# A Perceiver layer's scan: a sixth state pair summed on GpSimd, the gated sum behind the third keys, the first pair's products a step later

## The reference, cut to what matters

```
x = x + xattn(layernorm(x), ctx)            # softmax attention, 257 context tokens
h = layernorm(x)
gate = sigmoid(h @ W_gate.T + b_gate)
x_p, delta = split(h @ W_in.T + b_in);  delta = relu(delta)
s[t] = s[t-1] * exp(A * delta[t]) + x_p[t] * delta[t] * B     # 16 states, 512 channels
y[t] = s[t] @ C[0] + x_p[t] * D
x = x + (gate * y) @ W_out.T + b_out
```

## Time and profile before

| | us |
|---|---|
| median of 3 runs | 2247.94 (2247.15 to 2249.84) |
| the profiled execution | 2246.96 |
| its span in the trace | 2245.1 |
| granted PE clock, mean | 0.917 |

### The profile page before, as it was taken

The page is one execution under the profiler, slowest core; times in us unless marked ns, Lnnn a source line. Parts: engine busy times, 40 slices in busy tenths (PEclk is TensorE's granted clock), DMA queues, the critical chain, the costliest instruction groups (busy, mean ns, idle before and its releaser), DMA issues. The chain is left out here.

```text
span 2245.1 us, 41621 instructions
## 1 busy us (share of the span) xinstructions
PE 1864.1 (83%) x14355; PEld 1256.0 (56%) x14355; DVE 1592.2 (71%) x2945; ACT 1475.6 (66%) x3431; POOL 1207.8 (54%) x1300
## 2 busy tenths in 40 slices
PE   4898988988988898899899774378989898888964
PEld 2655555555555555555555432356666666676743
DVE  3348777767867867867858787457788878878763
ACT  2558877777868868867868776124666666656654
POOL 1435555545546545545545633156777767767751
PEclk8999999999999999999999997678889999989876
DMA  7321112112211211111111110100000000000000
GB/s 187 111 90 60 62 55 67 60 54 67 66 56 59 78 59 62 60 61 60 59 52 60 38 47 5 54 7 9 13 12 12 12 12 12 12 12 12 10 8 10
DMA packets 48370, 103.20 MB, mean 46 GB/s; under 512 B 6384, under 2 KB 25072, under 8 KB 43376
## 3 DMA queue, kind: packets, MB, share of 16 engines
q1 hardware_dynamic: 48240, 101.57, 14.4%
HBM read 93.03 MB, written 8.52 MB: 45 GB/s over the span
## 5 line engine op out<-in xcount | busy, mean ns | idle before, releaser
L861 POOL TENSOR_TENSOR kcube<-kcube,ksq 128x512 f32<-128x512 f32 x128 | 178.0, 1391 | 487.2 <-ACT ksq L718 487.2
L696 ACT ACTIVATE abuf<-delta,cols 128x496 f32<-128x496 f32 x512 | 337.6, 699 | 30.5 <-DVE gP L943 19.0
L871 POOL TENSOR_TENSOR yac<-yac,gP 128x1024 f32<-128x1024 f32 x128 | 301.7, 2357 | 11.4 <-ACT gP L705 10.3
L943 DVE TENSOR_TENSOR_SCAN gP<-abuf,ps_s 128x512 f32<-128x512 f32 x256 | 293.3, 1196 | 0.6 <-POOL yac L871 0.6
L943 DVE TENSOR_TENSOR_SCAN gL<-abuf,ps_s 128x512 f32<-128x512 f32 x192 | 223.2, 1206 | 57.7 <-ACT abuf L696 57.6
L583 PE MATMUL ps_kv<-hT,w_pT 128*128 128x512 f32 x384 | 194.0, 630 | 75.0 <-ACT delta L769 72.5
L512 PE MATMUL ps_kv<-w_k,cT 128*128 128x256 f32 x1024 | 256.1, 393 | 0.0
L524 PE MATMUL ps_kv<-kcube,cx 128*128 128x256 f32 x1024 | 246.8, 385 | 9.4 <-ACT kcube L736 8.6
L524 PEld LDWEIGHTS ps_kv<-kcube,cx 128*128 128x128 f32 x1024 | 192.7, 192 | 62.5 <-ACT kcube L736 20.3
L512 PEld LDWEIGHTS ps_kv<-w_k,cT 128*128 128x128 f32 x1024 | 184.7, 190 | 49.4 <-issue 29.4
L570 PE MATMUL ps_t<-gL,diag 128*128 128x512 f32 x384 | 184.7, 605 | 15.4 <-DVE gL L943 13.1
(11 more groups left out here) (312 smaller groups left out, 4279.8 us busy)
## 6 DMA issues: line engine op xcount, KB each, us to landing
cT<-in_h_ctxT SPq DMA_DIRECT2D x32, 1028.0 KB, 4.9
cx<-in_ctx SPq DMA_DIRECT2D x32, 1024.0 KB, 5.3
xT<-in_h_xT SPq DMA_DIRECT2D x8, 512.0 KB, 3.9
xcur<-in_x SPq DMA_DIRECT2D x32, 128.0 KB, 2.0
x_mid<-xb SPq DMA_DIRECT2D x16, 256.0 KB, 2.2
x_c<-x_mid SPq DMA_DIRECT2D x32, 128.0 KB, 2.0
out<-y SPq DMA_DIRECT2D x32, 128.0 KB, 1.7
kv_all<-vleft SPq DMA_DIRECT2D x8, 256.0 KB, 11.1
```

Of the source, the lines that this page charges most:

```text
L696: act.activation(abuf[q % 2][:, i, :].rearrange("p (b t) -> p b t", t=T)[:, :, 1:T], delta[J % 2][:, :].rearrange("p (b t) -> p b t", t=T) ...
L861: pool.tensor_tensor(t[:, :, :], t[:, :, :], ksq[:, :, :], ALU.mult).then_inc(S["k3_ready"], 1)
L871: pool.tensor_tensor(yac[:, :, :], yac[:, :, :], pool_home(q)[:, :, :], ALU.add).then_inc(S["pacc_done"], 1)
L943: dve.tensor_tensor_scan(dst[:, i, :], abuf[q % 2][:, i, :], ps_u[:, :], 0.0, ALU.mult, ALU.add).then_inc(S["scan_done"], 1)
```

## The change

- `BY_POOL` holds pair 6 too: six pairs on POOL, two (0 and 7) on PE. ACT scales pair 6 of Z between decay 0 and the squares of keys 0; POOL adds it behind the first cube.
- `yac` and `gate` have two buffers, used in turn. The waits of ACT's gate and of DVE's first scan on the last unit's gated sum are for the one before it.
- On DVE the gated sum of Z moves from behind pT to behind oT (after the third keys, ahead of scan 2), and `ks_added` moves ahead of scan 5.
- On PE the products of pair 0 run one step later, between the projections delta and x, instead of behind `pe_finish`.
- On POOL each addition comes one place earlier; the power `rstd1` now comes behind the second addition of J.

```diff
--- before.py
+++ after.py
@@ -29,7 +29,7 @@
 CB = EI // P
 NST = 16
 NPAIR = NST // 2
-BY_POOL = (1, 2, 3, 4, 5)
+BY_POOL = (1, 2, 3, 4, 5, 6)
 BY_PE = tuple(q for q in range(NPAIR) if q not in BY_POOL)
 NPE = len(BY_PE)
 NADD = len(BY_POOL)
@@ -184,11 +184,11 @@
 
         delta = [sb(f"delta{i}", [P, TS]) for i in range(2)]
         dx = sb("dx", [P, TS])
-        gate = sb("gate", [P, TS])
+        gate = [sb(f"gate{i}", [P, TS]) for i in range(2)]
         abuf = [sb(f"abuf{i}", [P, 2, TS]) for i in range(2)]
         gL = [sb(f"gL{i}", [P, 2, TS]) for i in range(2)]
         gP = [sb(f"gP{i}", [P, 2, TS]) for i in range(3)]
-        yac = sb("yac", [P, 2, TS])
+        yac = [sb(f"yac{i}", [P, 2, TS]) for i in range(2)]
         yg = sb("yg", [P, CB, TS])
 
         v = {**g, **locals()}
@@ -611,10 +611,10 @@
         if J is not None:
             pe_project(pe, "delta", J)
 
+        if Z is not None:
+            pe_states(pe, Z, 0)
         if J is not None:
             pe_project(pe, "x", J)
-        if Z is not None:
-            pe_states(pe, Z, 6)
         if C is not None:
             pe_gram(pe, C, 2)
 
@@ -655,8 +655,6 @@
             last.then_inc(S["oT_full"], 1)
         if C is not None:
             pe_finish(pe, C)
-        if J is not None:
-            pe_states(pe, J, 0)
         if g == 0 and sc >= 2:
             pe_out(pe, sc - 2, 0)
 
@@ -683,9 +681,9 @@
     def pe_home(J, q):
         return gL[(NPE * J + BY_PE.index(q)) % 2]
 
-    def pool_home(q):
+    def pool_home(J, q):
         k = BY_POOL.index(q)
-        return yac if k == 0 else gP[(k - 1) % 3]
+        return yac[J % 2] if k == 0 else gP[(k - 1) % 3]
 
     def act_decay(act, J, q):
         if q == 0:
@@ -699,7 +697,7 @@
 
     def act_weigh(act, J, q):
 
-        t = pool_home(q)
+        t = pool_home(J, q)
         for i in range(2):
             act.wait_ge(S["scan_done"], NST * J + 2 * q + i + 1)
             last = act.activation(t[:, i, :], t[:, i, :], ACT.Copy, scale=w_st[:, J % CB, 2 * q + i:2 * q + i + 1])
@@ -787,6 +785,8 @@
             act.activation(dx[:, :], ps_p, ACT.Identity, bias=db_x[:, J % CB:J % CB + 1],
                            scale=d_vec[:, J % CB:J % CB + 1]).then_inc(S["pj_act"], 1)
             act_decay(act, J, 0)
+        if Z is not None:
+            act_weigh(act, Z, 6)
         if A is not None:
             act_square(act, A, 0, True)
 
@@ -806,9 +806,9 @@
 
         if J is not None:
             act.wait_ge(S["pj_full"], filled("gate", J))
-            if J:
-                act.wait_ge(S["yg_ready"], J)
-            act.activation(gate[:, :], ps_p, ACT.Tanh, bias=b_gh[:, J % CB:J % CB + 1], scale=0.5).then_inc(S["pj_act"], 1)
+            if J >= 2:
+                act.wait_ge(S["yg_ready"], J - 1)
+            act.activation(gate[J % 2][:, :], ps_p, ACT.Tanh, bias=b_gh[:, J % CB:J % CB + 1], scale=0.5).then_inc(S["pj_act"], 1)
         if A is not None:
             act_square(act, A, 1, False)
         if J is not None:
@@ -865,22 +865,24 @@
         pool.wait_ge(S["scaled"], NADD * J + k + 1)
         if k == 0:
             pool.wait_ge(S["pj_act"], act_took("x", J))
-            pool.tensor_tensor(yac[:, 0, :], yac[:, 0, :], dx[:, :], ALU.add).then_inc(S["pacc_done"], 1)
+            pool.tensor_tensor(yac[J % 2][:, 0, :], yac[J % 2][:, 0, :], dx[:, :], ALU.add).then_inc(S["pacc_done"], 1)
         else:
             pool.wait_ge(S["pacc_done"], NADD * J + k)
-            pool.tensor_tensor(yac[:, :, :], yac[:, :, :], pool_home(q)[:, :, :], ALU.add).then_inc(S["pacc_done"], 1)
+            pool.tensor_tensor(yac[J % 2][:, :, :], yac[J % 2][:, :, :], pool_home(J, q)[:, :, :], ALU.add).then_inc(S["pacc_done"], 1)
 
     def pool_step(pool, G):
         A, C, J, Z = stages(G)
         g, sc = G % SG, G // SG
+        if Z is not None:
+            pool_add(pool, Z, 4)
         if C is not None:
             pool_ratio(pool, C, 1)
         if Z is not None:
-            pool_add(pool, Z, 4)
+            pool_add(pool, Z, 5)
         if A is not None:
             pool_cube(pool, A, 0)
         if Z is not None:
-            pool_add(pool, Z, 5)
+            pool_add(pool, Z, 6)
         if A is not None:
             pool_cube(pool, A, 1)
             pool_ratio(pool, A, 0)
@@ -888,17 +890,17 @@
             pool_add(pool, J, 1)
         if A is not None:
             pool_cube(pool, A, 2)
+        if J is not None:
+            pool_add(pool, J, 2)
+        if A is not None:
             pool.wait_ge(S["x_var"], A + 1)
             pool.tensor_tensor(rstd1[:, :], ve1[:, :], nhalf[:, 0:1], ALU.pow).then_inc(S["x_rstd"], 1)
         if J is not None:
-            pool_add(pool, J, 2)
+            pool_add(pool, J, 3)
         if A is not None:
             pool_cube(pool, A, 3)
             if A + 1 < NG:
                 pool_rstd0(pool, A + 1)
-        if J is not None:
-            pool_add(pool, J, 3)
-        if A is not None:
             if sc >= 2 and g % 2 == 0:
                 pool.wait_ge(S["x_out"][g // 2], 16 * (sc - 1))
             pool.tensor_tensor(xb[sc % 2][:, g, :], xcur[A % 2][:, :], bout[:, :], ALU.add).then_inc(S["xb_ready"], 1)
@@ -929,9 +931,10 @@
                 dve.wait_ge(S["y_full"], NPE * J + k - 1)
         else:
             k = BY_POOL.index(q)
-            dst = pool_home(q)
-            if k == 0 and J:
-                dve.wait_ge(S["y_summed"], J)
+            dst = pool_home(J, q)
+            if k == 0:
+                if J >= 2:
+                    dve.wait_ge(S["y_summed"], J - 1)
             elif k >= 4:
                 dve.wait_ge(S["pacc_done"], NADD * J + k - 2)
             elif k and J:
@@ -1000,6 +1003,20 @@
                 dve.wait_ge(S["pv_full"], A)
             dve.tensor_copy(pT[:, :], ps_m[:, 0:3 * P]).then_inc(S["pT_ready"], 1)
 
+        if A is not None:
+            dve.wait_ge(S["pv_full"], A + 1)
+            if A:
+                dve.wait_ge(S["oT_full"], A)
+            dve.tensor_scalar(o_sb[:, :], ps_m[:, 0:D], rinv[:, 0:1], None, ALU.mult).then_inc(S["o_ready"], 1)
+        if J is not None:
+            dve_scan(dve, J, 1)
+
+        if A is not None:
+            dve_keys(dve, A, 2)
+            dve.wait_ge(S["oT_full"], A + 1)
+            if A:
+                dve.wait_ge(S["o_full"], A)
+            dve.tensor_copy(oT[:, :, :], b3(ps_m[:, 0:D], DC)).then_inc(S["oT_ready"], 1)
         if Z is not None:
             dve.wait_ge(S["y_full"], NPE * (Z + 1))
             dve.wait_ge(S["pacc_done"], NADD * (Z + 1))
@@ -1007,26 +1024,12 @@
             if Z >= CB:
                 dve.wait_ge(S["pj_full"], filled("wo", 2 * (Z // CB - 1) + 1))
             out = yg[:, Z % CB, :]
-            dve.tensor_tensor(out, ps_y[:, :], yac[:, 0, :], ALU.add).then_inc(S["y_read"], 1)
+            dve.tensor_tensor(out, ps_y[:, :], yac[Z % 2][:, 0, :], ALU.add).then_inc(S["y_read"], 1)
             dve.wait_ge(S["y_read"], Z + 1)
-            dve.tensor_tensor(out, out, yac[:, 1, :], ALU.add).then_inc(S["y_summed"], 1)
+            dve.tensor_tensor(out, out, yac[Z % 2][:, 1, :], ALU.add).then_inc(S["y_summed"], 1)
             dve.wait_ge(S["y_summed"], Z + 1)
-            dve.scalar_tensor_tensor(out=out, in0=gate[:, :], scalar=1.0, in1=out, op0=ALU.add,
+            dve.scalar_tensor_tensor(out=out, in0=gate[Z % 2][:, :], scalar=1.0, in1=out, op0=ALU.add,
                                      op1=ALU.mult).then_inc(S["yg_ready"], 1)
-        if A is not None:
-            dve.wait_ge(S["pv_full"], A + 1)
-            if A:
-                dve.wait_ge(S["oT_full"], A)
-            dve.tensor_scalar(o_sb[:, :], ps_m[:, 0:D], rinv[:, 0:1], None, ALU.mult).then_inc(S["o_ready"], 1)
-        if J is not None:
-            dve_scan(dve, J, 1)
-
-        if A is not None:
-            dve_keys(dve, A, 2)
-            dve.wait_ge(S["oT_full"], A + 1)
-            if A:
-                dve.wait_ge(S["o_full"], A)
-            dve.tensor_copy(oT[:, :, :], b3(ps_m[:, 0:D], DC)).then_inc(S["oT_ready"], 1)
         if J is not None:
             dve_scan(dve, J, 2)
 
@@ -1071,15 +1074,16 @@
                 dve.wait_ge(S["lnh_ready"], A)
             dve.scalar_tensor_tensor(out=nbias[:, :], in0=mv1[:, 0:1], scalar=-1.0, in1=rstd1[:, :], op0=ALU.mult,
                                      op1=ALU.mult).then_inc(S["nbias_ready"], 1)
+        if C is not None:
+            dve.wait_ge(S["kst_full"], C + 1)
+            sums = ps_m[:, 0:D].rearrange("p (c b k) -> p b c k", c=DC, b=GB)[:, :, :, 0]
+            ks = ks_all[:, C * GB:(C + 1) * GB, :]
+            dve.tensor_tensor(ks, ks, sums, ALU.add).then_inc(S["ks_added"], 1)
         if J is not None:
             dve_scan(dve, J, 5)
         if C is not None:
             kv = kv_all[:, C * GB:(C + 1) * GB, :, :].rearrange("p b c e -> p (b c) e")
             kvn = kvt[:, :, :, :].rearrange("p b c e -> p (b c) e")
-            dve.wait_ge(S["kst_full"], C + 1)
```

(29 more changed lines are left out.)

## The result

The changed kernel takes 2392.07 us (2385.52 to 2398.95, 4 runs) against 2247.55; the ratio is 1.0642 (1.0614 to 1.0671). The direction was forecast, the size was not: +144 us where +83 stood, and 2392 lies above the range's 2345. The profiled execution is the fastest of its four, 2385.52 us with a span of 2383.7. Its last gated sum starts at 1536.5, where the kernel before had it at 1392.5: 144.0 us of loss arise in the first loop. Between the two profiled executions the whole difference is 138.6 us, as the second loop, which is the same code, took 5.4 less in the changed kernel's.

What follows compares the result with a forecast made beforehand. No engine was full; waits between engines working through written orders bound the first loop's steps. 2246.96 us + 82 (ordinary steps) + 6 (output steps) - 5 (stretched projection) gave 2330 us, 3.7% slower; range for 8 in 10: 2280 to 2345.

Steps and rivals of the forecast that it cites:

- The ring: First loop, ordinary step of 37.42 us: scan 2 on DVE gates ACT's decay 4; moving scan 2 moves the step, 21 times.
- the gated sum: On DVE, directly ahead of scan 2 in its new place, it makes decay 4 wait: 3.0 us a step.
- Pair 6 on POOL: ACT's two scalings delay the copy of gram 2, then gram 3 and keys 2: 0.9 us a step; POOL's addition covered.
- The step's 3.9 us: An ordinary step gets 0.9 + 3.0 = 3.9 us longer, 41.3; bounds 2.0 and 4.5; 21 steps give +82.
- POOL's order: rstd1 behind an addition of 2.36 us still reaches DVE's nbias in time: taken as 0, bounds 0 to 0.3 a step.
- The output steps: Six steps with an output projection: PE waits for the later gated sum, 6 x 1.0 = +6 us, bounds 0 and 9.
- The stretched projection: Projection x took 3.58 us instead of 1.98 in three steps; PE's spare time would recover it: -5 us, bounds -5 and +5.
- Pair 0 a step later: Its 1.9 us of products move into PE's wait of 2.30 ahead of projection x: covered, nothing gained where they stood.
- Rival 2: Faster because PE was the bound: 1.9 us less in 27 steps, 51 us, 2196 us; chance 0.10.
- Rival 1: Slower, but less: the sum meets no POOL instruction or gram 3 has its bank in time, 2292 us; chance 0.20.

Runs made afterwards that it cites:

- e3: The changed kernel with the gated sum moved back behind pT, still with two buffers and six pairs on POOL: 2311.34 us, ratio to before 1.027.
- e4: The changed kernel with pair 6 back on PE, behind projection x, all changes of order kept: 2382.37 us, ratio to before 1.059.
- e1: The changed kernel with the power rstd1 on POOL ahead of the second addition of J again: 2341.42 us, ratio to before 1.0403.
- e2: The changed kernel with nbias computed by a tensor_scalar with one SBUF tensor input, same value and place: 2344.99 us, ratio to before 1.0426.
- e6: The changed kernel with rstd1 ahead of the second addition again and the gated sum behind pT in the six output-projection steps alone: 2323.72 us, ratio to before 1.0339.
- e7: The kernel before with only pair 0's products a step later, ahead of projection x: 2231.47 us, ratio to before 0.9923.
- e5: The changed kernel with five pairs on POOL, the gated sum behind pT and nbias with one SBUF tensor input: 2226.44 us, ratio to before 0.9907.

## Why the prediction missed the size

- *The ring, and the gated sum.* Right. Scan 2 directly behind the sum, decay 4 waiting 3.5 us, the sum's last instruction at 1.64. e3 measured 2.7 us a step where the sum was priced at 3.0.
- *Pair 6 on POOL.* Right: gram 3 waits for ACT's copy, 1.0 us a step; e4 measured 1.0. POOL's own load is not seen as a cost: `nbias` and the sum's last instruction are as slow with five pairs.
- *The step's 3.9 us.* Right, for what it covered: with `nbias` mended the ordinary step is 41.4 us (e1, e2), where 41.3 stood. e1's total of 2341 lies in the range, in part by luck: the output intervals cost 23 us where 6 stood, the six with queries 16 where 23 stood, and the unchanged second loop of its trace took 6 us more.
- *The step of the prediction that failed* is "POOL's order": "Behind an addition of 2.36 it ends at about 909.6: covered by a hair; bounds 0 to 0.3 a step, taken as 0". It was late by 0.26 us (the wait of `nbias`), within those bounds. The hair of cover was itself time in which `kv_all`, ahead of `nbias`, ran beside an addition: it took 0.75 to 0.79 us in 22 steps before and never more than 0.39 in the changed kernel, so DVE came sooner. But being late put `nbias` behind the start of the next addition, and it was blocked for all of it: 1.63 us a step on ACT, 47 to 51 us in all with what follows in the query steps and in four ordinary ones (2392.07 - 2341.42 and 2392.07 - 2344.99). I had just used that very mechanism for the gated sum, and did not ask it of the small instruction whose start I had moved.
- *The output steps*, priced at 1.0 each for PE's wait (bounds 0 and 9 for six): the six intervals behind an output projection cost 19.5 us and in e1 22.8. I priced the wait, and not the clock that fell with it; e6 shows both gone together. These are the second term that was too small, by 13 to 17 us.
- *The stretched projection*, -5. In e1 and e2 it came: no ordinary interval there is above 41.4 us, where the kernel before has three of 39.0, 1.6 above the others. In the changed kernel it was lost again, with four intervals 1.3 above the others, by another product at a low clock (gram 2, under e2).
- *Pair 0 a step later*, priced at nothing: in ordinary steps it is nothing (37.46 in e7), but it is worth 20 us in the output steps. There PE's queue ahead of the projection was on the path; I looked at the place it moved to, and at ordinary steps alone. In the changed kernel this gain was covered: PE stood 2.88 us for the sum in the same place. The six steps with queries lose 8.4 us by it (e7).
- *Rival 2* (faster, PE the bound) is out for ordinary steps. *Rival 1* (less than forecast) erred the wrong way.

What each part is worth, measured by taking it out of the changed kernel: the sum's place 81 us (e3), `nbias` 47 to 51 (e2, e1), pair 6 10 (e4). That is 137 to 141, where e5, with all three gone, is 166 below the changed kernel. So some 25 us go only if several are gone together. By the traces, with e2 for `nbias`, they lie in every kind of interval: 5 us in the ordinary ones, 7 in those with queries, 2 behind the output projections, 8 in the last four; no run takes them apart. What stays of the change is worth 20 us in its favour, of which pair 0's place alone gives 18 (e7).
